# Thirty-two word scatters without a wait for each pair, and the last two tiles normalized by DVE

## What is computed

```
scores = softmax(x @ gate_weight.T); topk_w, topk_idx = top_k(scores, 2)
act    = silu(x @ gate.T) * (x @ up.T)                # of each chosen expert
y      = sum over the two experts of  topk_w * (act @ down.T)
y      = y + silu(x @ shared_gate.T) * (x @ shared_up.T) @ shared_down.T
x      = layernorm(x + y)
```

## Time and profile before

| What | Value |
|---|---|
| Median of 3 runs | 2107.75 us (2102.79 to 2109.4) |
| The profiled execution's own time | 2106.78 us |
| Its span | 2104.9 us |
| PE busy | 1932.6 us, 92% |
| DVE, ACT, POOL busy | 50%, 34%, 18% |
[...]

### The profile page before, as it was taken

How to read it: one execution, slowest core, us unless ns; L and a number is a source line. 1 busy time by engine, 2 the same in 40 slices (tenths; PEclk the granted TensorE clock), 3 DMA queues, 4 the chain that set the end, 5 groups by cost and what they waited for, 6 DMA issues and landing times. The chain is left out here.

```text
span 2104.9 us, 32789 instructions
## 1 busy us (share of the span) xinstructions
PE 1932.6 (92%) x12124; PEld 1575.4 (75%) x12124; DVE 1044.6 (50%) x1836; ACT 711.8 (34%) x2275; POOL 386.6 (18%) x339
## 2 busy tenths in 40 slices
PE   8999888999999979999899999899979996999991
PEld 6777677788888757877678877677758874899990
DVE  5676753455555455333455556676755232222224
ACT  4555634344444422212221112444632211233332
POOL 2110100000000056000021100000104222644335
PEclk9999999999999989999999999999999998999995
DMA  7211051000000021000290001000015100644257
GB/s 236 59 42 42 1 193 47 1 1 1 1 1 1 1 106 60 0 0 0 92 388 6 1 31 41 1 1 1 2 46 185 66 0 0 240 136 154 80 112 204
DMA packets 73376, 135.89 MB, mean 65 GB/s; under 512 B 13457, under 2 KB 31761, under 8 KB 71185
## 3 DMA queue, kind: packets, MB, share of 16 engines
q1 hardware_dynamic: 47376, 96.28, 13.2%
q0 software_dynamic: 7888, 27.94, 4.5%
q10 hardware_dynamic: 17968, 9.71, 1.8%
HBM read 90.62 MB, written 43.29 MB: 64 GB/s over the span
## 5 line engine op out<-in xcount | busy, mean ns | idle before, releaser
L1470 PE MATMUL banks<-ternary_xth,ternary_wq 128*128 (+1 forms) x352 | 141.0, 401 | 5.3 <-DVE ternary_wq L1401 3.9
L1470 PE MATMUL banks<-ternary_xtl,ternary_wq 128*128 (+1 forms) x352 | 139.4, 396 | 0.0
L571 ACT ACTIVATE causal_pr<-banks,causal_nb 128x128 f32<-128x128 f32 x256 | 89.9, 381 | 52.3 <-DVE causal_nb L713 52.3
L97 PE MATMUL banks<-latent_vh,latent_cth 128*128 128x512 f32 x256 | 104.2, 407 | 3.5 <-DVE latent_ctl L1171 3.5
L97 PE MATMUL banks<-weights,expert_xgh 128*128 x312 | 104.8, 336 | 2.4 <-DVE expert_xgl L2083 2.4
L571 ACT ACTIVATE gqa_pr<-banks,gqa_nb 128x128 f32<-128x128 f32 x256 | 89.9, 382 | 45.5 <-DVE gqa_nb L713 45.5
L99 PE MATMUL banks<-weights,expert_xgl 128*128 x312 | 101.5, 325 | 0.0
L98 PE MATMUL banks<-weights,expert_xgh 128*128 x312 | 101.5, 325 | 0.0
L99 PE MATMUL banks<-latent_vh,latent_ctl 128*128 128x512 f32 x256 | 100.2, 391 | 0.0
L98 PE MATMUL banks<-latent_vl,latent_cth 128*128 128x512 f32 x256 | 100.1, 391 | 0.0
L1430 DVE TENSOR_TENSOR ternary_hf<-ternary_sg,banks 128x512 f32<-128x512 f32 x44 | 30.2, 687 | 135.5 <-issue 79.6
(11 more groups left out here) (462 smaller groups left out, 5538.4 us busy)
## 6 DMA issues: line engine op xcount, KB each, us to landing
x_slots<-decay_zeros SPq DMA_DIRECT2D x39, 256.0 KB, 4.6
y_slots<-decay_zeros SPq DMA_DIRECT2D x39, 256.0 KB, 4.9
y_slots<-expert_ys SPq DMA_DIRECT2D x39, 256.0 KB, 2.1
expert_xin<-x_slots SPq DMA_DIRECT2D x38, 256.0 KB, 2.9
weights_raw<-in_expert_experts SPq DMA_DIRECT2D x4, 2176.0 KB, 9.7
gqa_tw<-in_ternary_w ACTq DMA_DIRECT2D x4, 2112.0 KB, 10.7
ternary_raw<-in_ternary_w SPq DMA_DIRECT2D x11, 768.0 KB, 4.1
expert_raw<-in_expert_experts POOLq DMA_DIRECT2D x3, 2176.0 KB, 10.0
```

Of the source, the lines that this page charges most:

```text
L97: pe.matmul(out, wh, xh, start=first, stop=False, **kw)
L571: a = act.activation(pr[:, h, c, :], S.bank[2 * h + c // 4][:, (c % 4) * P:(c % 4 + 1) * P], ACT.Exp, bias=nb[:, h, c:c + 1], accum_out=su ...
L1470: a = pe.matmul(dst[:, :], wq[:, j, m, c * P:(c + 1) * P], x[:, c, toks], start=c == 0 and n == 0, stop=c == C - 1 and n == 1)
```

## The change

In `shared_ffn_phase` the wait before each pair of the weight scatters is gone; the wait for all 32 stays. In `expert_ffn_phase` tiles 14 and 15 are normalized by DVE, with one `tensor_scalar` each (subtract the mean, times `rs`), in place of ACT; SP's stores of these two wait on DVE's count. `shifts(2)` moves from the end of the turn n = 15 to that of n = 14. `shifts(3)` stays behind the loop. `shifts(4)` is no longer needed.

```diff
             for n in range(2 * B):
                 at = bass.IndirectOffsetOnAxis(ap=S.pos[:, n:n + 1], axis=0)
-                if n and n % 2 == 0:
-                    pool.wait_ge(scored, 16 * n)
                 pool.indirect_dma_start(S.s_slots, at, S.score[:, n:n + 1], None).then_inc(scored, 16)
             pool.wait_ge(scored, 16 * 2 * B)
...
+        last_done, BY_ACT = sem("last_done"), sets[-1][0]
...
             for t in range(B):
-                sp.wait_ge(x_done, t + 1)
+                if t < BY_ACT:
+                    sp.wait_ge(x_done, t + 1)
+                else:
+                    sp.wait_ge(last_done, t - BY_ACT + 1)
                 sp.dma_start(S.out_dram[:, t, :], S.X[:, t, :]).then_inc(stored, 16)
...
-            for k, (lo, hi) in enumerate(sets):
+            for k, (lo, hi) in enumerate(sets[:-1]):
                 act.wait_ge(shift_done, k + 1)
...
-                if n - 4 in ends:
+                if n - 4 in ends[:2]:
                     shifts(ends.index(n - 4))
-            for k in range(len(sets)):
-                if ends[k] + 4 >= B + 2:
-                    shifts(k)
+                if n == ends[2] + 3:
+                    shifts(2)
+            shifts(3)
+            dve.wait_ge(rs_done, len(sets))
+            for t in range(*sets[-1]):
+                dve.tensor_scalar(S.X[:, t, :], S.X[:, t, :], mv[:, t, 0:1], rs[:, t:t + 1],
+                                  ALU.subtract, ALU.mult).then_inc(last_done, 1)
```

## The result

The changed kernel's median is 2116.28 us (2109.96 to 2118.71, eight runs), against 2108.14 us (2102.79 to 2112.13, eight runs) of the kernel before: ratio 1.0034, 95% interval 1.0019 to 1.005. It is slower by 0.3%. The forecast was 2086. The record names no chip for these runs; for all later ones it does. The profiled execution took 2109.96 us, with a span of 2108.2, where before it took 2106.78 with 2104.9.

The account below looks back on a forecast made before the run. PE was taken as the bound at 92% busy, with POOL late at one block end, leaving PE idle 21.33 us. Terms 18.55 + 1.0 + 1.6 = 21.15 us, from the median 2107.75 to 2086 us, range 2081 to 2095.

Parts of the forecast that it names:

- The step that failed: Shared phase: POOL's denser word scatters from 1648 to 1689 us run beside a busy PE and cost nothing.
- rival C: Word scatters to neighbouring slots hinder each other, POOL reaches the block end later than now; up to 2128 us, chance 0.05.
- Landing of the word scatters: Shared phase: scatters served in turn, 3.24 us each; last lands at 1755.4, POOL arrives at 1760.7, 9.8 us before DVE.
- Rivals B: Landings slow with more in flight and still partly decide POOL's arrival at the block end; 2097.6 us, chance 0.09.
- D: POOL's drain, not the waits, holds it and grows to fill the time won; no gain, chance 0.02.
- Term 1, the block end: End of shared phase: DVE comes last instead of POOL, PE starts at 1772.47, not 1791.02; 18.55 us, at most 19.2.
- Term 2, the clock: Expert phase, tile 0: shorter PE gap lessens the slow clock's 3.0 us cost; gain 1.0 us, 0 to 3.0.
- Term 3, the tail: End of kernel: earlier shifts and DVE normalizing two tiles bring the last store sooner; 1.6 us, 0.8 to 1.9.

Follow-up runs that it names:

- e1: Changed kernel with the waits for pairs put back, so the new tail alone; 2111.13 against 2110.86 us of the kernel before, ratio 1.0003.
- the windows of two and four: Changed kernel with each word scatter waiting for the one two, or four, before it; 2086.63 us (0.9879) and 2085.84 us (0.9877) against the kernel before.
- e11: Changed kernel with the weights 64 bytes apart (16 words a slot), no waits for pairs; 2088.34 us, 0.9889 of the kernel before.
- e16: Changed kernel with the waits for pairs put back and the weights 64 bytes apart; 2086.11 against 2111.01 us of the kernel before, 0.9872.
- e9: Changed kernel unaltered, run again on chip 5; 2088.13 us, 0.9885 of the kernel before.
- e10: Changed kernel with each word scatter issued twice, the second to an array nobody reads, 64 in a row; 2086.12 us, 0.9881 of the kernel before.
- e2: Changed kernel with the old tail back, so only the waits for pairs are gone; 2091.33 us, 0.9902 of the kernel before.
- e17: Changed kernel unaltered, run again on chip 7; 2086.57 us, 0.9876 of the kernel before.

## Why the prediction was wrong, step by step

**The step that failed** is one sentence: "POOL's denser issues from 1648 to 1689 lie beside a busy PE, just as the x scatters did before them". I put the cost of the denser issues at nothing, because PE is busy meanwhile, and argued from x scatters, which are as dense and leave PE at full pace. On two of seven occasions it is not nothing: while POOL issues 32 word scatters in a row, DVE and ACT, and then PE, get their work late, from ten microseconds after the first scatter until shortly before the last has landed. It costs 23.7 us in the profiled execution, more than the 19.1 that the block end gives, and no part of the chain near the block end shows it. My rival C had the sign, but another mechanism (slow landings that hold POOL), and the traces refute that one: POOL was early in every one of them.

What clogs the issue is **open**. That the stretch comes of the row of word scatters is argued from its times, in two traces; it isn't shown. A rival stands: that such an occasion slows this phase whatever the waits. In the kernel before POOL comes 19.1 us behind DVE, so that a delay of PE and DVE of up to 19 us would be hidden, and no trace of that kernel is known to come from such an occasion. Its times speak only against a full stretch, and not strongly: PE would then start some 148 us after the first word scatter, where with the waits kept it is 143.23 (before) or 145.93 (e1), so 2 to 5 us would be added; on chip 9 that kernel took 2111.98 us, on chips 4, 5, 7 and 10 2110.86 to 2111.65. Nor does any run tell what the profiler's recording has to do with it: every run here was profiled, and what the two traces lack are mostly the records of POOL's scatters. It isn't DMA bandwidth (2% busy). That it isn't the tail, the number of scatters or the place of the array is shown only for chips that don't have it. Whether the windows of two and four or the layout of e11 and e16 escape it on a chip that has it wasn't tried.

**Landing of the word scatters.** "Served one behind the other at about 3.24 us each" was wrong, though harmless for the sum. At that rate the last would have landed at 1755; it had by 1694.1, 7.4 us after its issue, and in e9 the median landing is 7.0 with some six in flight. They overlap. What a landing took went with the layout: 2.1 us in the median with the words 64 bytes apart against 7.0 at 4 bytes (e11 against e9, same chip). The size of a write doesn't make this difference, since both layouts write 4 bytes at a time. But the array is also 16 times as large in e11, and no run separates its size from the distance. That neighbouring words take turns, which e11 was to test, was my estimate and isn't shown. Rivals B and D fall too: POOL's drain is the same 5.28 us as with two in flight; it was longer, 7.89 us, only where more were issued (e10), and the change left their number as it was.

**Term 1, the block end**, forecast 18.55: where the slow stretch is absent it holds. In e9 DVE ends at 1770.20 (1767.44 + 2.76) and PE starts 1.39 us later, where I had 1.93; with 0.34 from DVE's own earlier end the difference is 19.43 (0.34 + 0.54 + 18.55). The 0.34 is drift between executions; the term itself measured 19.1.

**Term 2, the clock**, forecast 1.0: tile 0 takes 8.66 us (1771.59 to 1780.25), tile 1 still 6.15; before it was 9.17. So 0.5 us came back, and 2.5 of the 3.0 stayed. In all sixteen traces of e2 to e17 the first two tiles together take 14.62 to 14.88 us, against 15.32 before, so the term is worth 0.4 to 0.7. PE stood still for 2.23 us, and the granted clock behind it, same columns as above, e9:

```profile
1769.00:1771.50 2.50, 0.36 (x2) 0.00 (x0) 1.20 (x2) 0.00 (x0) 0.00 (x0) 1.00 0.00 0
1772.00:1777.00 5.00, 3.38 (x13) 2.99 (x12) 0.69 (x1) 0.60 (x1) 0.00 (x0) 0.50 0.81 213
1777.00:1780.00 3.00, 3.00 (x16) 3.00 (x16) 0.00 (x0) 0.46 (x1) 0.00 (x0) 0.74 0.99 418
```

It was 1.00 until PE came back at 1771.59, 0.50 from 1772 to 1777, and rose within 1777 to 1780, where its mean is 0.74.

**Term 3, the tail**, forecast 1.6: the chain did what was forecast up to the last store. The end of the timeline in e9:

```profile
2074.29 4.34 ACT L2076 ACTIVATE X<-X,expert_shift,expert_rs 128x512 f32<-128x512 f32 x6 [1.52 <-DVE expert_shift L2109]
...
2076.84 0.70 POOL L2028 TENSOR_TENSOR expert_rs<-expert_ve,mhalf 128x2 f32<-128x2 f32 x1 [0.32 <-DVE expert_ve L2104]
2077.57 1.00 DVE L2133 TENSOR_SCALAR X<-X,expert_mv,expert_rs 128x512 f32<-128x512 f32 x2 [0.75 <-POOL expert_rs L2028]
```

ACT runs six tiles, DVE two in 1.00 us (forecast 1.1), and the last store starts at 2079.5, 2.0 us after POOL's last power (2077.54), where it was 4.0. But two things gave most of it back. The last store is passed as landed 2.6 us after its start (2079.5 to 2082.1), where it was 2.1 (2100.6 to 2102.7). The median over the sixteen shows the same:

```profile
out<-X SPq DMA_DIRECT2D x16, 256.0 KB, 2.4
```

against 2.1 in before and in e2, with the old tail. And the last power starts 290.44 us after tile 2's transposes, in place of 289.59 (2095.93 - 1806.34), 0.85 later where I had allowed 0.35. From tile 2 to the end of the span e9 is 0.46 us shorter. One trace against one can't weigh half a microsecond, though. In the sixteen traces with the whole new tail this stretch takes 297.43 to 298.71 us, 297.99 in the mean; in the two with the whole old tail 298.56 (before) and 298.84 (e2). By these the tail is worth some 0.7 us, less than half of the forecast. e1's times, with an interval of -2.1 to +3.4 us, agree with either.

The three measured terms, 19.43 + 0.51 + 0.46 = 20.4 us, are the difference between the spans, 2104.9 - 2084.5. Against the forecast 21.15 that is 0.75 too little. So the sum was right for the kernel in which nothing new happens, and its medians there, 2086.57 to 2090.82 us, lie in the range given; beside the kernel before on the same chips they are 16.3 to 24.4 us less. The range had no case for what took place in two of seven. Part of the agreement is luck: the block end gave more than forecast, the clock and the tail less.

**The version to take** is e16, waits for pairs kept and each weight in 64 bytes of its own: 0.9872, not to be told from the kernel without waits (0.9876, same chip), and it never has more small writes in flight than the kernel before. That this keeps it clear of the slow stretch is a guess: no run of it was made where the stretch is known to come.

## What to carry to other kernels

When a wait is removed, the rate at which the freed queue now issues is itself a change, and "it lies beside a busy engine" needs a row that shows that engine at full pace beside that kind of transfer, not beside a larger kind. A wait also hides what happens beside it: in the kernel before, up to 19 us of delay in PE would have left no mark on the time. A slow transfer is better asked why it is slow before its wait is dropped: here words 64 bytes apart, in an array 16 times as large, took the wait from 92.9 us to 22.0 and gave the same gain. And a gain or loss of 1% of a kernel on one chip should be seen on a second before the code is blamed for it.

## What the runs showed of the hardware that I had not expected

- The slow stretch: some 35 us (1657 to 1692) in which DVE and ACT, and from 1666 PE, get their work late while POOL issues at its normal 1.26 us. The times have it in all runs on two occasions and in none on five; the two traces of these occasions lack some 690 of 6800 landing records, from the first x scatters on.
- Small writes: 128 words of 4 bytes in a scatter landed in 7.0 us in the median with the slots 4 bytes apart (e9), and in 2.1 us at 64 bytes apart, in an array 16 times as large (e11). Distances between were not tried.
- POOL's drain behind the scatters took 5.28 us whether two were in flight (before, e16) or more (e9), and whether they landed in 7.0 or 2.1 us (e9, e11); with 32 more issues it took 7.89 (e10).
- One of the word scatters took POOL 5.02 us to issue, in place of 0.96. The timelines of POOL and DVE in e9:

```profile
1681.69 0.96 POOL L1626 DMA_INDIRECT s_slots<-score,pos  x1 [0.30 <-issue]
1682.96 5.02 POOL L1626 DMA_INDIRECT s_slots<-score,pos  x1 [0.30 <-issue]
```

```profile
1682.45 4.69 DVE L1680 TENSOR_TENSOR weights<-weights_raw,weights 128x4352 fp32r<-128x4352 f32 x1 [5.99 <-ACT weights L1645]
```

It began 0.51 us behind the start of DVE's subtraction over 4352 columns, and ended 0.84 us behind its end at 1687.14. In before one took 4.30 us, from 1684.05, and ended 0.84 us behind the end of the same subtraction (1682.82 + 4.69). In the changed kernel's first trace a short one of DVE's operations with both inputs in SBUF (L1787, 1654.57 to 1655.26) goes with a scatter that took 1.47 us, from 1654.62, and ended 0.83 us behind it. So the issue of a scatter seems to have waited for DVE. All three of these operations of DVE read both inputs from SBUF, where the scatter's indices, `S.pos`, lie too. Whether it was the reading of the indices that waited or another part of the issue, no run here separates.
